# The loads of a head pair issued later, the mask adds split off, and a pair of context tiles kept in SBUF

## The chip, the cores and the metric

The kernel runs on one core of a Trainium2 chip. The time is the device time of one execution in microseconds (us); lower is better.

## What is computed

Sixteen sequences of 64 tokens with 512 features go through LayerNorm and a cross-attention over a context of the same shape (32 heads of 128), with a position bias and a mask, then a residual; then LayerNorm, a base linear map plus eight low-rank experts weighted by a router, and a residual.

```python
q = (layernorm(x) @ Wq).reshape(16, 64, 32, 128)      # k, v: ctx @ Wk, ctx @ Wv
score = einsum('bqhd,bkhd->bhqk', q, k) / sqrt(128) + position_bias
probs = softmax(where(mask, score, -inf))             # masked places are 0
x = x + einsum('bhqk,bkhd->bqhd', probs, v).reshape(16, 64, 4096) @ Wo
h = layernorm(x); w = topk weights of softmax(h @ router_W.T + router_b), by expert_map
x = x + h @ base_W.T + base_b + 2 * sum_e w_e * (h @ A_e.T) @ B_e.T
```

## The kernel before

**Arithmetic.** TensorE (PE) multiplies in a reduced format. So each fp32 operand is split into a high and a low part, and each product is three matmuls: high by high, high by low, low by high. ScalarE (ACT) makes the high parts (`wk_hi`, `co_hi`, `wo_hi`), VectorE (DVE) the low ones (`wk_lo`, `co_lo`, `wo_lo`). On top of this stands the Strassen-Winograd scheme: a block of two heads is computed as seven products, `times(n, p)` with p = 1, 2, 6, 7, 5, 3, 4, of six matmuls 128x512 each. The sums that the scheme wants of the weights are made by GpSimd (POOL) in `sums_of_b(w)` (four operations into `twk`/`twv`), those of the activations by DVE in `sums_of_a(j)` (into `sums_c`, `sums_x`).

**Stages.** Blocks n = 0 to 15 make V and are stored in HBM, blocks 16 to 31 make K likewise. From block 31 on come the Q blocks. Then sixteen rounds over pairs of heads follow (i = 0 to 15). In each, PE first does what this text calls the group of small passes: transposing the probabilities of the old pair (`turn_p`), scores of the next one (`scores`, L1544) and probabilities by V (`times_v`, L1569, output `pO`, `pT_`, `pS`). These are some 190 short matmuls with 4-byte operands. Then it does the products of Q block n = i + 33 mixed with eight output tiles `times_wo(i, t)` into `pY`, which DVE adds to the residual `y` (`add_tile`, L1101):

```python
for p in (1, 2, 6, 7): times(n, p)
times_wo(i, 0); times_wo(i, 1); times(n, 5); times_wo(i, 2); times_wo(i, 3)
times(n, 3); times_wo(i, 4); times_wo(i, 5); times(n, 4); times_wo(i, 6); times_wo(i, 7)
```

`times_wo(i, t)` with t of 2 or more waits until tile t - 2 has been added (`y_added`), because `pY` has two buffers. The engines meet only through semaphores; each engine's own order is the order in which the code is written.

**DVE in a round.** Bias and row maximum (`biased`, `largest`, `less_max`), low parts of the attention output (`oT_lo`), the row sums and scaled probabilities (`add_up`, L1131; `weights`, L1133 to L1140, whose L1135 and L1140 read two SBUF operands), the `q` combinations (L897, L903, L908), low weights (L887), and the eight `add_tile`.

**POOL in a round.** `sums_of_b(i + 22)` and then `add_mask` for the two heads of the pair after next (L581), each waiting for its bias load.

**SP in a round.** The loads, in the order `wo_raw` (after `wo_l`), `k` (after `s_full`: the scores have read the old k), eight bias pieces (each four after `s_read`), `wk_raw`, and `v` (after `o_full`: `times_v` has read the old v).

**Opening.** The eight context tiles are transposed in pairs (`turn_pair(j)`, with `rows_out(j)` on ACT making the high and low copies). The sums for index 0 (`sums_of_a(0)`) are made late, at block 5; by then the PSUM copy of tiles 0 and 4 is gone, so PE transposes them again at n = 5 (`turn(ctx[:, 0, :], ...)`, L1429), and `rows_out(0)` copies them. `ORDER` lists the first products.

**End.** Before the last pair's `times_v`, PE transposes the last weights of the FFN (`ffn_weights(6)`, L1619, `b_raw`).

## Time and profile before

| | us |
|---|---|
| median of 3 runs | 797.49 (796.79 to 798.37) |
| the profiled execution, whole | 799.1 |
| its span on the core | 797.3 |
| PE busy in the span | 781.9 (98%) |
| DVE busy | 585.0 (73%) |
| ACT busy | 335.4 (42%) |
| POOL busy | 186.6 (23%) |

The span runs from the first to the last instruction of the core; the whole execution has a little around it. Busy time counts an engine's own work, overlaps within the engine counted once. The profile of one execution gives the start and length of each instruction, and, in brackets, how long its engine had been idle and which instruction released it.

### The profile page before, as it was taken

To read this page: it belongs to the slowest core of one execution; us is meant where nothing else is said; L and a number is where in the kernel's file an instruction comes from. 1 tells how busy PE (TensorE), PEld (TensorE's weight loads), DVE (VectorE), ACT (ScalarE), POOL (GpSimd) and SP (SyncE) were. 2 spreads that over 40 slices of the span, in tenths; PEclk is the share of its full clock that TensorE was granted. 3 is DMA by queue.
4 is the path that set the end of the run, shared out by engine and by line. 5 is a ranking of instruction groups with operands and counts; after the bars stand their busy time and mean duration, and the time that the engine had idled before them with its cause. 6 is when DMAs were issued, how large, how long until landed. Compare 5 with 4: busy or idle time off the path is not lost.

```text
span 797.3 us, 16339 instructions
## 1 busy us (share of the span) xinstructions
PE 781.9 (98%) x6368; PEld 651.8 (82%) x6368; DVE 585.0 (73%) x1047; ACT 335.4 (42%) x657; POOL 186.6 (23%) x203
## 2 busy tenths in 40 slices
PE   9999999999999999989999999999999999999998
PEld 7788888888888888768888878887888788888886
DVE  6794626267677666688987888788878887869884
ACT  5563525245455555452443234423443343324420
POOL 0134041024334334242212221212221221010200
PEclk9999999999999999999999999999999999999999
DMA  6536674234544556583564355435543455344002
GB/s 224 196 121 211 214 238 145 106 142 159 186 163 159 164 165 211 168 245 107 159 186 114 103 163 179 126 105 159 170 144 114 141 160 167 93 121 101 1 3 105
DMA packets 108075, 118.35 MB, mean 148 GB/s; under 512 B 44240, under 2 KB 77008, under 8 KB 107999
## 3 DMA queue, kind: packets, MB, share of 16 engines
q1 hardware_dynamic: 107998, 117.31, 46.7%
q8 instruction: 51, 0.84, 0.4%
q14 instruction: 26, 0.20, 0.1%
HBM read 81.64 MB, written 35.65 MB: 147 GB/s over the span
## 4 chain that ended last, share of the span: by engine, by line
PE 89%; DVE 7%; DMA 2%; issue 1%; SPq 1%; ACT 0%; DVEq 0%
PE pY L1383 40%; PE pP L1383 36%; PE pY L1544 4%; PE pO L1569 2%; PE pT_ L1569 1%; DVE pr L1140 1%; DVE rs L1135 1%; DVE y L1101 1%; DVE sm L1131 1%; PE pO L1383 1%; PE pT_ L1554 1%; PE pS L1554 1%; DMA k_hbm<-stage 1%; DMA v<-v_hbm 1%; SPq L422 1%
## 5 line engine op out<-in xcount | busy, mean ns | idle before, releaser
L1383 PE MATMUL pY<-wo_hi,oT_hi 128*128 128x512 f32 x248 | 97.8, 394 | 3.6 <-DVE y L1101 2.3
L1101 DVE TENSOR_TENSOR y<-y,pY 128x512 f32<-128x512 f32 x124 | 84.7, 683 | 18.6 <-PE pY L1383 18.3
L1383 PE MATMUL pY<-wo_lo,oT_hi 128*128 128x512 f32 x248 | 96.7, 390 | 0.0
L1383 PE MATMUL pY<-wo_hi,oT_lo 128*128 128x512 f32 x248 | 96.6, 390 | 0.0
L1383 PE MATMUL pP<-xo_hi,wk_hi 128*128 128x512 f32 x210 | 83.7, 398 | 1.8 <-ACT v_s L633 0.8
L648 ACT CAST wk_hi<-twk 128x256 fp32r<-128x256 f32 x128 | 52.1, 408 | 72.6 <-PE pP L1383 61.1
L1383 PE MATMUL pP<-xo_lo,wk_hi 128*128 128x512 f32 x210 | 81.9, 390 | 0.0
L1383 PE MATMUL pP<-xo_hi,wk_lo 128*128 128x512 f32 x210 | 81.9, 390 | 0.0
L581 POOL TENSOR_TENSOR bias<-bias,madd 128x512 f32<-128x512 f32 x32 | 42.7, 1348 | 151.8 <-DMA bias<-in_fside_Bx32xSxS 151.8
L887 DVE TENSOR_TENSOR wk_lo<-twk,wk_hi 128x256 fp32r<-128x256 f32 x128 | 58.8, 464 | 23.3 <-ACT wk_hi L648 23.3
L887 DVE TENSOR_TENSOR wk_lo<-wk_raw,wk_hi 128x256 fp32r<-128x256 f32 x96 | 46.6, 486 | 21.9 <-ACT wk_hi L648 21.8
L1383 PEld LDWEIGHTS pY<-wo_hi,oT_hi 128*128 128x128 f32 x248 | 46.5, 188 | 16.4 <-DVE y L1101 5.7
L564 POOL TENSOR_TENSOR twk<-wk_raw 128x256 f32<-128x256 f32 x32 | 24.5, 764 | 129.1 <-DVE wk_lo L887 104.2
L1383 PEld LDWEIGHTS pY<-wo_lo,oT_hi 128*128 128x128 f32 x248 | 46.5, 188 | 9.8
L1383 PEld LDWEIGHTS pY<-wo_hi,oT_lo 128*128 128x128 f32 x248 | 46.6, 188 | 9.2
L575 POOL TENSOR_TENSOR twk<-wk_raw,twk 128x256 f32<-128x256 f32 x32 | 24.0, 749 | 117.7 <-DVE wk_lo L887 117.7
L1383 PEld LDWEIGHTS pP<-xo_hi,wk_hi 128*128 128x128 f32 x210 | 39.4, 188 | 12.9 <-issue 4.4
L633 ACT COPY v_s<-pP 128x512 f32<-128x512 f32 x31 | 18.2, 587 | 75.2 <-PE pP L1383 75.2
L1383 PE MATMUL pP<-co_hi,wk_hi 128*128 128x512 f32 x126 | 49.3, 391 | 0.0
L1383 PE MATMUL pP<-co_lo,wk_hi 128*128 128x512 f32 x126 | 49.0, 389 | 0.0
L1383 PE MATMUL pP<-co_hi,wk_lo 128*128 128x512 f32 x126 | 49.0, 389 | 0.0
L1383 PEld LDWEIGHTS pP<-xo_lo,wk_hi 128*128 128x128 f32 x210 | 39.4, 188 | 8.4
(277 smaller groups left out, 1916.9 us busy)
## 6 DMA issues: line engine op xcount, KB each, us to landing
v_hbm<-stage SPq DMA_DIRECT2D x64, 256.0 KB, 2.3
k_hbm<-stage SPq DMA_DIRECT2D x64, 256.0 KB, 3.5
k<-k_hbm SPq DMA_DIRECT2D x16, 1024.0 KB, 5.4
v<-v_hbm SPq DMA_DIRECT2D x16, 1024.0 KB, 7.3
wk_raw<-in_L_xattn_Wk SPq DMA_DIRECT2D x16, 512.0 KB, 4.4
wo_raw<-in_L_xattn_Wo SPq DMA_DIRECT2D x16, 512.0 KB, 3.7
bias<-in_fside_Bx32xSxS SPq DMA_DIRECT2D x128, 64.0 KB, 3.5
wk_raw<-in_L_xattn_Wq SPq DMA_DIRECT2D x16, 512.0 KB, 4.6
```

The lines of the kernel that those rows point to most:

```text
L422: sp.dma_start(bias[h % 2][64 * f:64 * f + 64, i::2, :], bias_d[f, i, h]).then_inc(ld_bias[h % 2], 16)
L564: nc.gpsimd.tensor_tensor(tw[:, 0, :, :], raw_block(w, 1, 1), raw_block(w, 0, 1), ALU.subtract).then_inc(tw_made, 1)
L575: nc.gpsimd.tensor_tensor(tw[:, 3, :, :], raw_block(w, 1, 0), tw[:, 1, :, :], ALU.subtract).then_inc(tw_made, 1)
L581: nc.gpsimd.tensor_tensor(b[:, :, :], b[:, :, :], madd[:, :, :], ALU.add).then_inc(bias_made, 1)
L633: nc.scalar.copy(v_s[:, :], x_bank(n)[:, :]).then_inc(v_made, 1)
L648: nc.scalar.copy(w_part(w, 0)[:, slot, :, :], w_source(w, slot)).then_inc(w_hi[slot], 1)
L887: nc.vector.tensor_tensor(dst, src, hi.bitcast(F32), ALU.subtract).then_inc(done, 1)
L1101: nc.vector.tensor_tensor(y[:, t, :], y[:, t, :], src[:, :], ALU.add).then_inc(y_added, 1)
L1383: mm = nc.tensor.matmul(bank_, a, b, start=first and n == 0, stop=last and n == len(terms) - 1, skip_group_check=read_between)
L1544: mm = nc.tensor.matmul(pY[s][64 * half:64 * half + 64, blk * S:(blk + 1) * S], q[:, s, b * S:(b + 1) * S], k[:, s, b * S:(b + 1) * S], st ...
L1554: mm = nc.tensor.transpose(pT_of[h % 2][:, j * P:(j + 1) * P], pr[h % 2][:, 2 * j:2 * j + 2, :].rearrange("p a k -> p (a k)"), ident[:, :])
L1569: mm = nc.tensor.matmul(pO_of[s][i][64 * d:64 * d + 64, t * S:(t + 1) * S], v[rows, t, s * DH + 64 * d:s * DH + 64 * d + 64], pT[s][rows, ...
```

## The change

The change moves work and takes a little of it away; the arithmetic is the same.

1. **Opening.** Product 5 of block 1 goes ahead of product 2 of block 2, and the DVE and ACT operations for them change places with it.
2. **Tiles 0 and 4.** Their transposed form is copied from PSUM to SBUF (`kept0`, two ACT copies) when it is first made. The second transposing (8 PE transposes), and `rows_out(0)`, go. `turn_pair(2)` waits for the copies.
3. **Before the rounds.** ACT does `copy_c12` ahead of `exp(0)`, DVE `make_c11` ahead of `weights(0)`.
4. **SP.** In a round, `wo_raw` comes first; everything else waits for `o_full`, that is for the end of the group of small passes; then `wk_raw`, the bias, `k`, `v`.
5. **POOL.** The two `add_mask` stand between the third and fourth operation of `sums_of_b`.
6. **wo.** ACT makes `wo_high(i + 1)` two steps earlier, and DVE makes `lower_wo(i + 1)` right after `add_tile(i, 1)` where it stood after `add_tile(i, 4)`.
7. **End.** `ffn_weights(6)` and its split stand behind the last pair's `times_v`.

```diff
--- before.py
+++ after.py
@@ -81,7 +81,7 @@
-ORDER = [(1, 1), (0, 2), (1, 2), (0, 4), (0, 3), (0, 7), (1, 6), (1, 7), (2, 1), (2, 2), (1, 5), (1, 3), (2, 6),
+ORDER = [(1, 1), (0, 2), (1, 2), (0, 4), (0, 3), (0, 7), (1, 6), (1, 7), (2, 1), (1, 5), (2, 2), (1, 3), (2, 6),
          (2, 7), (1, 4), (2, 5)]
 for n_ in range(3, QA + 1):
...
@@ -91,10 +91,9 @@
 DONE = {step: i + 1 for i, step in enumerate(ORDER)}
-FIRST_TURN = [0, 1, 4, 6, 10, 12, 14, 16]
-SECOND_TURN = [2, 3, 5, 7, 11, 13, 15, 17]
-AGAIN = (8, 9)
-NTURN = 18
+FIRST_TURN = [0, 1, 4, 6, 8, 10, 12, 14]
+SECOND_TURN = [2, 3, 5, 7, 9, 11, 13, 15]
+NTURN = 16
 SUM_ORDER = [1, 2, 3, 0, 4, 5, 6, 7]
@@ -200,6 +199,8 @@
         low = [at("low_c", R2, [P, DC, P]), at("low_x", R4 + 6144, [P, DC, P])]
         sums_a = [at("sums_c", R2 + 2048, [P, 4, 2, P]), at("sums_x", R4 + 8192, [P, 4, 2, P])]
+        kept0 = [at("kept0_a", R2 + 6144, [P, 2, 2, P]), at("kept0_b", R2 + 8192, [P, DC, P])]
+
         R5 = R4 + 24576
         twv = at("twv", R5, [P, 4, 2, HALF])
@@ -510,15 +511,16 @@
...
                 sp.wait_ge(wo_l, i + 1)
                 load_wo(i + 1)
+
+                sp.wait_ge(o_full, 4 * (i + 1))
+                if i + 24 < NSET:
+                    load_wk(i + 24)
                 if i + 2 < NP:
-                    sp.wait_ge(s_full, 2 * i + 4)
-                    load_k(i + 2)
                     for s in range(2):
                         sp.wait_ge(s_read, 2 * i + 3 + s)
                         load_bias(2 * i + 4 + s)
-                if i + 24 < NSET:
-                    load_wk(i + 24)
-                sp.wait_ge(o_full, 4 * (i + 1))
+                    sp.wait_ge(s_full, 2 * i + 4)
+                    load_k(i + 2)
                 load_v(i + 1)
                 if i == NP - 4:
@@ -553,7 +555,12 @@
                 b = n % NX
                 nc.gpsimd.tensor_tensor(rstd[:, b:b + 1], ve[:, b:b + 1], mhalf[:, :], ALU.pow).then_inc(rstd_made, 1)
-            def sums_of_b(w):
+            def add_mask(h):
+                pool.wait_ge(ld_bias[h % 2], 64 * (h // 2 + 1))
+                b = bias[h % 2]
+                nc.gpsimd.tensor_tensor(b[:, :, :], b[:, :, :], madd[:, :, :], ALU.add).then_inc(bias_made, 1)
+
+            def sums_of_b(w, masks=()):
                 tw = tw_of(w)
                 wait_raw(pool, w)
@@ -570,15 +577,12 @@
...
                 nc.gpsimd.tensor_tensor(tw[:, 2, :, :], raw_block(w, 0, 1), raw_block(w, 0, 0), ALU.subtract
                                         ).then_inc(tw_made, 1)
+                for h in masks:
+                    add_mask(h)
                 pool.wait_ge(w_lo[6], w)
                 pool.wait_ge(tw_made, 4 * w + 2)
                 nc.gpsimd.tensor_tensor(tw[:, 3, :, :], raw_block(w, 1, 0), tw[:, 1, :, :], ALU.subtract
                                         ).then_inc(tw_made, 1)
-
-            def add_mask(h):
-                pool.wait_ge(ld_bias[h % 2], 64 * (h // 2 + 1))
-                b = bias[h % 2]
-                nc.gpsimd.tensor_tensor(b[:, :, :], b[:, :, :], madd[:, :, :], ALU.add).then_inc(bias_made, 1)
             for n in range(QA + 1):
                 if n in (1, 5, 9):
@@ -594,11 +598,12 @@
                     rstd_of((n - 16) // 3 * 2 + 1)
             for i in range(NP):
+                heads = (2 * i + 2, 2 * i + 3) if i + 1 < NP else ()
                 if i + 22 < NSET:
-                    sums_of_b(i + 22)
-                if i + 1 < NP:
-                    add_mask(2 * i + 2)
-                    add_mask(2 * i + 3)
+                    sums_of_b(i + 22, heads)
+                else:
+                    for h in heads:
+                        add_mask(h)
             pool.wait_ge(ld_small, 48)
             for t in range(NT):
...
@@ -697,15 +702,21 @@
...
             higher(0, 2)
             piece_of_first(1, 3, pP[0], c12_made)
+
+            act.wait_ge(a21_l, 1)
+            nc.scalar.copy(kept0[0][:, :, :, :], first_turn(0)[:, :].rearrange("p (k c t) -> p k c t", k=2, c=2)
+                           ).then_inc(kept0_made, 1)
+            nc.scalar.copy(kept0[1][:, :, :], second_turn(0)[:, :].rearrange("p (c t) -> p c t", c=DC)
+                           ).then_inc(kept0_made, 1)
             piece_of_first(3, 7, pP[1], c22_made)
             first_high(2)
+            higher(0, 4)
             copy_u(1)
             rows_out(2)
             last_high(2)
-            higher(0, 4)
             copy_p1(2)
+            sums_high(2)
             copy_v(1)
-            sums_high(2)
             higher(0, 6)
             copy_c12(1)
...
@@ -736,8 +747,6 @@
...
                 if j is not None:
                     sums_high(j)
-                if n == 5:
-                    rows_out(0)
                 copy_v(n)
                 if n == 5:
...
@@ -792,8 +801,8 @@
...
             copy_v(n)
             higher(w, 4)
+            copy_c12(n)
             exp(0)
-            copy_c12(n)
             higher(w, 5)
             exp(1)
...
@@ -831,10 +840,10 @@
...
                 copy_u(n)
                 higher_of(w, 2)
+                wo_high(i + 1)
                 higher_of(w, 3)
                 copy_v(n)
                 higher_of(w, 4)
-                wo_high(i + 1)
                 copy_c12(n)
                 higher_of(w, 5)
...
@@ -854,9 +863,9 @@
...
             turned_p(h + 3)
             split_ffn(5)
-            split_ffn(6)
             o_high(h + 2)
             o_high(h + 3)
+            split_ffn(6)
             for i in range(NT + 1):
                 if i < NT:
@@ -925,7 +934,12 @@
                 low_, s, k = low[j // 4], sums_a[j // 4], SUM_ORDER.index(j)
                 one = first_turn(j)[:, :].rearrange("p (k c t) -> p k c t", k=2, c=2)
-                dve.wait_ge(low_made, k + 1)
+                if j == 0:
+                    one, low_ = kept0
+                    dve.wait_ge(kept0_made, 2)
+                else:
+
+                    dve.wait_ge(low_made, k + 1 if j < 4 else k)
                 if k >= 1:
                     dve.wait_ge(as_lo, k)
...
@@ -1029,13 +1043,13 @@
...
             lower_w(0, 2)
             make_c11(1)
-            first_low(2)
             first_t1()
             first_t4()
+            first_low(2)
             lower_w(0, 4)
             sums_of_a(2)
+            sums_low(2)
             make_c11(2)
-            sums_low(2)
             lower_w(0, 6)
             make_c22(1)
...
@@ -1180,9 +1194,9 @@
...
             add_up(0)
             lower_w(w, 6)
+            make_c11(n)
             weights(0)
             lower_w(w2, 0)
-            make_c11(n)
             add_up(1)
             lower_w(w2, 1)
...
@@ -1217,6 +1231,7 @@
...
                 weights(h + 3)
                 add_tile(i, 1)
+                lower_wo(i + 1)
                 lower_of(w, 1)
                 lower_of(w, 2)
...
@@ -1226,7 +1241,6 @@
...
                 lower_of(w, 5)
                 add_tile(i, 4)
-                lower_wo(i + 1)
                 add_tile(i, 5)
                 make_c21(n)
...
@@ -1436,8 +1450,7 @@
             def turn_pair(j):
                 if j == 2:
-                    pe.wait_ge(a6_lo, 1)
-                    pe.wait_ge(a21_l, 1)
+                    pe.wait_ge(kept0_made, 2)
                 elif j == 4:
                     pe.wait_ge(as_lo, 4)
...
@@ -1499,8 +1512,8 @@
...
             times(1, 7)
             times(2, 1)
+            times(1, 5)
             times(2, 2)
-            times(1, 5)
             times(1, 3)
             times(2, 6)
...
@@ -1514,10 +1527,6 @@
...
                 if prep_at(n) is not None:
                     turn_pair(prep_at(n))
-                if n == 5:
-                    pe.wait_ge(a6_lo, 3)
-                    turn(ctx[:, 0, :], first_turn(0))
-                    turn(ctx[:, 4, :], second_turn(0))
                 times(n, 6)
                 times(n, 7)
...
@@ -1677,9 +1686,9 @@
...
             turn_p(h + 3)
             ffn_weights(5)
-            ffn_weights(6)
             times_v(h + 2)
             times_v(h + 3)
+            ffn_weights(6)
             def turn_last(t):
                 pe.wait_ge(xn2_made, t + 1)
```

Three places show how the rows move. SP's queue in the second round, before: the loads that serve the pair after this one.

```order
L426 DMA wo_raw<-in_L_xattn_Wo 128x2x512 [waits wo_l]
L429 DMA k<-k_hbm 128x2x1024 [waits s_full]
L422 DMA bias_92<-in_fside_Bx32xSxS_0 64x4x64 [waits s_read]
L422 DMA bias_92<-in_fside_Bx32xSxS_0 64x4x64 x3
L422 DMA bias_93<-in_fside_Bx32xSxS_0 64x4x64 [waits s_read]
L422 DMA bias_93<-in_fside_Bx32xSxS_0 64x4x64 x3
L416 DMA wk_raw_99<-in_L_xattn_Wq 128x4x256 [waits tw_made,w_lo5]
L432 DMA v<-v_hbm 128x8x256 [waits o_full]
```

The same place on SP in the changed kernel.

```order
L427 DMA wo_raw<-in_L_xattn_Wo 128x2x512 [waits wo_l]
L417 DMA wk_raw_99<-in_L_xattn_Wq 128x4x256 [waits tw_made,w_lo5,o_full]
L423 DMA bias_92<-in_fside_Bx32xSxS_0 64x4x64 [waits s_read]
L423 DMA bias_92<-in_fside_Bx32xSxS_0 64x4x64 x3
L423 DMA bias_93<-in_fside_Bx32xSxS_0 64x4x64 [waits s_read]
L423 DMA bias_93<-in_fside_Bx32xSxS_0 64x4x64 x3
L430 DMA k<-k_hbm 128x2x1024 [waits s_full]
L433 DMA v<-v_hbm 128x8x256
```

`wk_raw` now goes ahead of the bias, `k` behind it, and all of them behind the wait for `o_full`.

On POOL, the sums of one weight set and the masks of one pair, before:

```order
L564 TENSOR_TENSOR twk<-wk_raw_98 128x256 [waits w_lo3,ld_wk0]
L568 TENSOR_TENSOR twk<-twk,wk_raw_98 128x256 [waits tw_made,w_lo2]
L571 TENSOR_TENSOR twk<-wk_raw_98 128x256 [waits w_lo4]
L575 TENSOR_TENSOR twk<-wk_raw_98,twk 128x256 [waits tw_made,w_lo6]
L581 TENSOR_TENSOR bias_92<-bias_92,madd 128x512 [waits ld_bias0]
L581 TENSOR_TENSOR bias_93<-bias_93,madd 128x512 [waits ld_bias1]
```

The same place on POOL in the changed kernel:

```order
L571 TENSOR_TENSOR twk<-wk_raw_98 128x256 [waits w_lo3,ld_wk0]
L575 TENSOR_TENSOR twk<-twk,wk_raw_98 128x256 [waits tw_made,w_lo2]
L578 TENSOR_TENSOR twk<-wk_raw_98 128x256 [waits w_lo4]
L561 TENSOR_TENSOR bias_92<-bias_92,madd 128x512 [waits ld_bias0]
L561 TENSOR_TENSOR bias_93<-bias_93,madd 128x512 [waits ld_bias1]
L584 TENSOR_TENSOR twk<-wk_raw_98,twk 128x256 [waits tw_made,w_lo6]
```

The fourth sum now stands behind both masks.

On DVE, the middle of a round before, from the second `add_tile` on (`y<-y,pY` is an `add_tile`, `q<-pP,v_s` is `make_c22`):

```order
L1101 TENSOR_TENSOR y<-y,pY 128x512 [waits y_full]
L887 TENSOR_TENSOR wk_lo<-wk_raw_99,wk_hi 128x256 [waits w_hi1]
L887 TENSOR_TENSOR wk_lo<-twk,wk_hi 128x256 [waits w_hi2]
L903 TENSOR_TENSOR q<-pP,v_s 128x512 [waits s_full,v_made,prod]
L887 TENSOR_TENSOR wk_lo<-twk,wk_hi 128x256 [waits w_hi3]
L1101 TENSOR_TENSOR y<-y,pY 128x512 [waits y_full]
L887 TENSOR_TENSOR wk_lo<-twk,wk_hi 128x256 [waits w_hi4]
L1101 TENSOR_TENSOR y<-y,pY 128x512 [waits y_full]
L887 TENSOR_TENSOR wk_lo<-wk_raw_99,wk_hi 128x256 [waits w_hi5]
L1101 TENSOR_TENSOR y<-y,pY 128x512 [waits y_full]
L887 TENSOR_TENSOR wo_lo_56<-wo_raw,wo_hi_55 128x1024 [waits wo_h]
```

The same place on DVE in the changed kernel:

```order
L1115 TENSOR_TENSOR y<-y,pY 128x512 [waits y_full]
L896 TENSOR_TENSOR wo_lo_56<-wo_raw,wo_hi_55 128x1024 [waits wo_h]
L896 TENSOR_TENSOR wk_lo<-wk_raw_99,wk_hi 128x256 [waits w_hi1]
L896 TENSOR_TENSOR wk_lo<-twk,wk_hi 128x256 [waits w_hi2]
L912 TENSOR_TENSOR q<-pP,v_s 128x512 [waits s_full,v_made,prod]
L896 TENSOR_TENSOR wk_lo<-twk,wk_hi 128x256 [waits w_hi3]
L1115 TENSOR_TENSOR y<-y,pY 128x512 [waits y_full]
L896 TENSOR_TENSOR wk_lo<-twk,wk_hi 128x256 [waits w_hi4]
L1115 TENSOR_TENSOR y<-y,pY 128x512 [waits y_full]
L896 TENSOR_TENSOR wk_lo<-wk_raw_99,wk_hi 128x256 [waits w_hi5]
```

`wo_lo` has moved from behind the fifth `add_tile` of the round to a place ahead of the third.

## Rows read from the trace of the kernel before

**Rows 1.** PE alone: one round, then twelve. Length, busy (count), clock, DMA share, GB/s.

```profile
402.69:428.24 25.55, 25.55 (x292) 1.00 0.50 145
376.39:690.75 314.36, 310.00 (x3482) 1.00 0.47 141
```

**Rows 2.** PE alone: 13 groups of small passes, the same columns; the sum of all.

```profile
402.69:406.73 4.04, 4.04 (x194) 1.00 0.17 23
...
663.67:668.81 5.14, 4.24 (x193) 1.00 0.36 102
...
sum 55.88, PE 53.88; mean PE 4.14
```

**Rows 3.** Timeline: PE resumes in the longest group (start, length, idle before).

```profile
668.67 0.21 PE L1569 MATMUL pS<-pT,v 64*64 64x64 f32 x1 [0.90 <-issue]
```

**Rows 4.** The page's instruction queue (packets, MB), and a stretch of all engines.

```profile
q8 instruction: 51, 0.84, 0.4%
...
665.87:665.97 0.10, 0.10 (x17) 0.10 (x16) 0.10 (x1) 0.00 (x0) 0.00 (x0) 1.00 0.70 164
```

**Rows 5.** Timeline: SP's queue in round 376.39.

```profile
378.51 0.37 SPq L429 DMA_DIRECT2D k<-k_hbm  x1
378.93 5.71 SPq L422 DMA_DIRECT2D bias<-in_fside_Bx32xSxS  x8
```

**Rows 6.** Timeline: POOL, DVE and PE in round 376.39.

```profile
385.94 2.53 POOL L581 TENSOR_TENSOR bias<-bias,madd 128x512 f32<-128x512 f32 x2 [9.84 <-DMA bias<-in_fside_Bx32xSxS]
385.97 1.27 DVE L1135 TENSOR_TENSOR rs<-rs,some 128x8 f32<-128x8 f32 x1
387.28 1.74 DVE L1140 TENSOR_TENSOR pr<-pr,rs 128x512 f32<-128x512 f32 x1
390.71 0.50 PE L1383 MATMUL pY<-wo_hi,oT_hi 128*128 128x512 f32 x1 [0.46 <-DVE y L1101]
```

**Rows 7.** Timeline: the same engines in round 402.69.

```profile
411.55 1.29 POOL L581 TENSOR_TENSOR bias<-bias,madd 128x512 f32<-128x512 f32 x1 [9.15 <-DMA bias<-in_fside_Bx32xSxS]
412.90 0.69 DVE L1140 TENSOR_TENSOR pr<-pr,rs 128x512 f32<-128x512 f32 x1
418.20 0.68 DVE L1101 TENSOR_TENSOR y<-y,pY 128x512 f32<-128x512 f32 x1
420.47 0.39 PE L1383 MATMUL pY<-wo_hi,oT_hi 128*128 128x512 f32 x1
```

**Rows 8.** Durations of wo_lo: ns min/median/max, first and last start.

```profile
L887 DVE TENSOR_TENSOR wo_lo<-wo_raw,wo_hi x16: 1219/1220/1760, 346.1 to 735.7; 128x1024 fp32r<-128x1024 f32 x16
```

**Rows 9.** Timeline of the opening.

```profile
31.73 0.47 PE L1383 MATMUL pY<-wv_hi,co_hi 128*128 128x512 f32 x1 [0.77 <-ACT v_s L633]
32.56 1.23 DVE L887 TENSOR_TENSOR co_lo<-sums_c,co_hi 128x1024 fp32r<-128x1024 f32 x1 [1.07 <-ACT co_hi L673]
32.96 0.40 PE L1383 MATMUL pY<-wv_lo,co_hi 128*128 128x512 f32 x1
33.89 0.47 PE L1383 MATMUL pP<-wv_hi,co_hi 128*128 128x512 f32 x1 [0.54 <-issue]
```

**Rows 10.** Timeline: tiles 0 and 4 transposed again, and what follows.

```profile
64.87 0.60 PE L1429 MATMUL pS<-ident,ctx 128*128 128x128 f32 x4
...
65.66 0.48 PE L1383 MATMUL pY<-wv_hi,co_hi 128*128 128x512 f32 x1
```

**Rows 11.** Timeline ahead of the rounds and in the first.

```profile
336.16 0.47 PE L1383 MATMUL pP<-xo_hi,wk_hi 128*128 128x512 f32 x1 [0.53 <-ACT stage L638]
...
341.07 0.47 PE L1383 MATMUL pP<-xo_hi,wk_hi 128*128 128x512 f32 x1 [0.48 <-DVE q L897]
...
351.22 0.29 PE L1569 MATMUL pO<-pT,v 64*64 64x64 f32 x4 [0.17 <-DMA v<-v_hbm]
...
354.88 0.50 PE L1383 MATMUL pP<-xo_hi,wk_hi 128*128 128x512 f32 x1
```

**Rows 12.** Timeline of the end.

```profile
740.00 0.47 PE L1383 MATMUL pY<-wo_hi,oT_hi 128*128 128x512 f32 x1 [1.12 <-issue]
```

More of the change, by code:

```diff
@@ L287, in xattn_ffn @@
         turned, turned_hi, turned_lo = sem("turned"), sem("turned_hi"), sem("turned_lo")
-        low_made, sum_step = sem("low_made"), sem("sum_step")
+        low_made, sum_step, kept0_made = sem("low_made"), sem("sum_step"), sem("kept0_made")
         a01_hi, a01_lo, a6_hi, a6_lo = sem("a01_hi"), sem("a01_lo"), sem("a6_hi"), sem("a6_lo")
@@ L474, in _ @@
                     for t in range(NT):
-                        sp.wait_ge(turned, 10)
+                        sp.wait_ge(turned, 8)
                         sp.dma_start(y[:, t, :], x_d[:, t, :]).then_inc(ld_x[t], 16)
@@ L656, in rows_out @@
             def rows_out(j):
-                act.wait_ge(turned, AGAIN[1] + 1 if j == 0 else SECOND_TURN[j] + 1)
+                act.wait_ge(turned, SECOND_TURN[j] + 1)
                 if j != 1:
@@ L987, in normalise @@
                     if m >= NX:
-                        dve.wait_ge(turned, 10 + m - NX + 1)
+                        dve.wait_ge(turned, 8 + m - NX + 1)
                     nc.vector.tensor_scalar(xn[:, b, :], y[:, t, :], mv[:, b, 0:1], rstd[:, b:b + 1],
```

## The prediction

> **What bounds the kernel now.** I read first the stretches of PE, since PE is the engine that is hardly ever idle. In twelve rounds, 314.36 us, it is busy for 310.00 [rows 1]. So only work taken off PE, or a wait of PE that goes, can shorten the time; DVE, ACT, POOL and the DMA queues count only where PE stands waiting for them. The granted clock is 1.00 in each of these stretches, so nothing is lost or to be won there. The round without any wait takes 25.55 [rows 1]. Twelve of those would be 306.60, so the twelve rounds hold 314.36 - 306.60 = 7.76 of waiting. Where is it?
>
> The second view is the groups of small passes. The undisturbed one issues its first part in 4.04, thirteen of them take 55.88 against 13 x 4.04 = 52.52 [rows 2]: 3.36 too much, of which 0.34 belongs to the thirteenth, after the twelve rounds. So about 3.0 of the 7.76 sits in the groups and 4.7 outside. The timeline of the rest shows the second kind in round 376.39: `wo_hi,oT_hi` at 390.71 starts after PE has been idle for 0.46, released by an addition to `y` on DVE [rows 6]. Seven of the twelve rounds have such waits.
>
> Why is `y` late? POOL adds the masks from 385.94 on for 2.53; DVE's L1135, an operation on 8 columns, starts beside it at 385.97 and takes 1.27, and L1140 takes 1.74 [rows 6]. In round 402.69 the mask comes at 411.55, after L1135, L1140 takes 0.69, and PE waits for no `y` [rows 7]. So a mask add that lies beside a DVE operation with two SBUF inputs holds it up, by up to 1.05 (1.74 - 0.69), and `add_tile(0)` and what follows are late.
>
> **Opening.** Matmuls of a product start 0.23 apart: from 31.73 to 32.96 there are five steps, the first of them 0.30 [rows 9]. A matmul shown with 0.40 thus overlaps the next by 0.17, and a wait costs its idle time, 0.17, and 0.07 for the slower first step. Two waits stand here: 0.77 for `v_s`, and one of 0.54 behind which `co_lo` (32.56 + 1.23 = 33.79) is what ends last [rows 9]. With the 0.24 each they cost 1.01 and 0.78. The new order puts product 5, whose inputs are there, into this place, and both should go: -1.8. The kept copies are two ACT operations of some 0.6 each; they fall where ACT waits for PE, before the next transposing. Were they not hidden they would cost 1.2, which is the bound. The eight transposes at n = 5 go: from 64.87 to 65.66 is 0.79 [rows 10], and with what the switch costs the next product (0.08) this is -0.9.
>
> **Before the rounds.** The waits at 336.16 (0.53, for ACT's `stage`) and 341.07 (0.48, for DVE's `q`) [rows 11] cost 0.77 and 0.72, together 1.5; ACT and DVE now do the copy and the `q` first. But `v` arrives only just ahead of 351.22, and from there to the next product at 354.88 lie 3.66 of small passes [rows 11], which a late `v` would hold in place. I take -1.3, between 0.3 (the `v` load stays where it is, only the queue behind it shortens) and 1.6.
>
> **The loads in the rounds.** `k` is issued at 378.51, inside the group (2.12 after its start), then eight bias pieces in 5.71, some 0.71 each [rows 5]. Now all of this waits for the end of `times_v`. Nobody needs `k` before the next round's scores, 25.55 after, so being late costs nothing by itself. What could it win? The 3.36 in the groups. Only every third group is long, although `k` is issued at the same place in each. In the longest, PE resumes at 668.67 after 0.90 without a releaser [rows 3], 2.7 after a short burst of the DMA engines (0.70 busy in 0.1 us) ended at 665.97. The instruction queue brings 0.84 MB in 51 packets, 16.5 KB each [rows 4]. The other long groups end 2.5 to 2.8 after such a burst as well, at whatever other traffic. I read this as PE's own code arriving late, on a rhythm set by the number of instructions, and take 0 from the loads. The bounds are -3.4, if the loads were what delays the code, and +1, if 16 fewer PE instructions move the rhythm into a worse place.
>
> The Trainium skill, "Runtime: NRT & Kernel Launch", section "Instruction fetch mechanics", says that code comes in 16 KiB blocks of 256 instructions, that PE holds 128 KiB, and that crossing a block is mostly hidden. The packet size here agrees with the block; by "mostly hidden" the gaps would need another cause, the loads would be the first suspect, and the sum would be lower by the 3.4 of the row; by the rows I leave it out.
>
> **The masks.** With the bias starting 2.5 after the group's start, the masks came 9.5 (385.94 - 376.39) and 8.9 (411.55 - 402.69) after it [rows 6, 7]. Now the group must end (4.04 at least, [rows 2]) and `wk_raw` goes first (about 0.5), so the bias starts some 2.0 later and the first mask lands 10.9 to 11.6 after the start, the second 1.5 later. `weights(h + 2)` on DVE ends at 412.90 + 0.69, which is 10.9 after the start: the first pair of DVE operations is free, and the second (`weights(h + 3)`) can still be met. That would clear most of the 4.7. But there is a new load on DVE ahead of the third addition: `wo_lo`, 1.22 [rows 8]. In the clean round that addition ends at 418.20 + 0.68 = 418.88, and PE wants it at 420.47 [rows 7]: a margin of 1.59, of which 0.37 is left. One contention of 1.05 against 0.37 makes 0.68 of waiting, and I expect it in something under half of the rounds: 0.3 a round, 3.6 in twelve. Against 4.7 that is -1.1. The lower bound is no waits at all, -4.7; the upper is in the rivals. The fourth POOL sum, now behind the masks, feeds weights that DVE takes later in the round, past the tile additions. ACT's earlier `wo_high` is work that ACT, 42% busy, has room for; that `wo_raw` is free earlier only lets its load go earlier.
>
> **End.** `ffn_weights(6)` before `times_v` is four transposes, about 0.45; behind them PE waits 1.12 at 740.00 anyway [rows 12]. Moved into that wait they are free: -0.45.
>
> **The sum.** -1.8 - 0.9 - 1.3 + 0 - 1.1 - 0.45 = -5.55. The profiled execution took 799.1 (span 797.3), so it would take 793.5; it lies 1.6 above the median of the runs, and the same edits on the median of 797.49 give **791.9**.
>
> **The rivals.**
>
> *A, the loads do delay the code.* For it: the longest group has the DMA engines busy for 0.36 of its time, the short ones 0.17 [rows 2]. Against it: in a longer window more of `k` is bound to show, and two of three groups pass with the same issues. It takes a further 3.4: 788.5; with clean additions too, 784.9.
>
> *B, the masks meet DVE, and `wo_lo` has eaten the margin.* Ends on the other side. If the bias lands sooner than I think, so that the first mask begins before 9.8 after the group's start, where `weights(h + 2)` has its turn, both L1135 and L1140 are held (1.1 and 1.05, [rows 6]). Before, this cost up to 26.3 - 25.55 = 0.75 a round; now a further 1.22 stands in front of the third addition. I price it at 1.2 a round, between 0.75 and 0.75 + 1.22. Twelve rounds give 14.4 for 4.7, +9.7 in place of -1.1: 797.49 - 4.45 + 9.7 = 802.7. It decides the sign from 4.7 + 4.45 = 9.15 in twelve rounds, 0.76 a round. Against it: the 2.0 by which the chain of issues moves is sure, except in the last rounds, which have no `wk_raw` ahead.
>
> *C, the gains of opening and setup are given back.* Another input, DVE's low weights or `v`, ends the same waits a little later: half of 1.8 and 1.0 of the 1.3 go, and masks still cost what they did (1.1): 791.9 + 3.0 = 794.9; with the kept copies in the way (1.2), 796.1.
>
> **How the numbers follow.** Forecast 0.50, with a range of its own of 790 to 793.9; A 0.17; C 0.18, of which a third ends within 0.2% of before; B 0.15, of which a fifth ends within 0.2%. A measurement of this kernel can tell 0.2%, 1.6 us, from no change. Faster than 795.9: 0.50 + 0.17 + 0.12 = 0.79, less 0.03 for terms that miss together: 0.76. Within: 0.06 + 0.03 + 0.03 = 0.12. Slower than 799.1: 0.12. The range takes in most of A (down to 786.5) and C and its neighbours (up to 798); B above it and the far end of A are left out.
>
> **What would show it.** Opening: no PE wait longer than 0.2 between the products of blocks 1 and 2, and the start of the K blocks earlier by 2.7. The transposes at n = 5 missing. Rounds: first mask 10.9 to 11.6 after the group's start, L1140's successor near 0.69 for the first head, PE's waits for `y` adding up to 3 to 4 in twelve rounds, most of them ahead of the fifth tile. Groups: every third still long by 0.4 to 1.1, 2.5 to 2.8 after a 16.5 KB burst; if they are all 4.04 long, A holds and my reading of the code fetch is wrong. End: the wait at 740.00 shorter by the four transposes. The prediction fails high if `wo_lo` proves to be waited for in every round, and low if the groups go clean.

## The result, and the profile after

The changed kernel is slower: 805.13 us median (804.93 to 807.83, 4 runs) against 797.22 of the kernel before beside it, a ratio of 1.0105, 95% interval 1.0081 to 1.0129. Forecast was 791.9, with a range up to 798.0. The profiled execution has a span of 803.4.

The page: busy time of the engines, and the first matmuls of the output tiles (the last column is PE's idle time ahead of them and what ended it).

```profile
PE 782.9 (97%) x6360; PEld 649.8 (81%) x6360; DVE 586.2 (73%) x1047; ACT 334.9 (42%) x658; POOL 198.7 (25%) x203
...
L1397 PE MATMUL pY<-wo_hi,oT_hi 128*128 128x512 f32 x248 | 99.2, 400 | 7.4 <-DVE y L1115 6.6
```

The engines do the same work, but PE now waits 7.4 ahead of its output tiles, 6.6 of it for `y`. The stretches of PE (start and end, length, busy (count), clock, DMA share, GB/s): the twelve rounds, and of thirteen groups of small passes some, with their sum.

```profile
374.01:694.80 320.79, 312.58 (x3481) 1.00 0.45 138
...
374.01:378.05 4.04, 4.04 (x193) 1.00 0.02 4
...
507.73:512.75 5.02, 4.36 (x194) 1.00 0.02 5
...
694.80:699.43 4.63, 4.30 (x194) 1.00 0.01 4
sum 55.69, PE 53.71; mean PE 4.13
```

Against [rows 1] the twelve rounds take 320.79 - 314.36 = 6.43 more. Against [rows 2] the groups take 55.69 for 55.88: nothing changed there, although the DMA engines now stand nearly still in them (4 to 8 GB/s where there were 18 to 102). So the loss is between the groups. The span reads as follows, against the kernel before: up to the first scores 327.69 for 330.60, -2.91; from there to the first of the twelve rounds 46.32 for 45.79, +0.53; twelve rounds +6.43; round 14 26.17 for 25.88, +0.29; from 720.97 to the end 82.43 for 80.67, +1.76. The sum is 6.1, the difference of the spans.

One of the rounds, that of 481.17, by timeline (POOL, DVE, then PE):

```profile
490.50 1.30 POOL L561 TENSOR_TENSOR bias<-bias,madd 128x512 f32<-128x512 f32 x1 [15.20 <-DMA bias<-in_fside_Bx32xSxS]
490.75 1.07 DVE L1149 TENSOR_TENSOR rs<-rs,some 128x8 f32<-128x8 f32 x1
494.21 1.73 POOL L561 TENSOR_TENSOR bias<-bias,madd 128x512 f32<-128x512 f32 x1 [2.41 <-DMA bias<-in_fside_Bx32xSxS]
495.30 1.72 DVE L896 TENSOR_TENSOR wo_lo<-wo_raw,wo_hi 128x1024 fp32r<-128x1024 f32 x1
495.90 1.72 POOL L584 TENSOR_TENSOR twk<-wk_raw,twk 128x256 f32<-128x256 f32 x1
496.95 0.95 DVE L896 TENSOR_TENSOR wk_lo<-wk_raw,wk_hi 128x256 fp32r<-128x256 f32 x1
499.09 0.68 DVE L1115 TENSOR_TENSOR y<-y,pY 128x512 f32<-128x512 f32 x1
499.82 0.50 PE L1397 MATMUL pY<-wo_hi,oT_hi 128*128 128x512 f32 x1 [0.71 <-DVE y L1115]
```

The reader is to see three meetings. The first mask meets L1149 (the former L1135), 9.3 after the group's start, where I had forecast 10.9 to 11.6. The second mask meets `wo_lo`, and so does the fourth POOL sum behind it: `wo_lo` takes 1.72 where 1.22 is its length alone [rows 8]. The same sum then meets `wk_lo`, which takes 0.95 for 0.42. Behind all this stands the third addition (499.09), and PE waits for it ahead of the fifth output tile. In the kernel before, seven of the twelve rounds have a wait for `y`, all ahead of the third or fourth tile and none ahead of the fifth. Now 13 rounds (the first to the thirteenth) wait ahead of the fifth, with PE idle for 0.14 to 0.94, and three of them also ahead of the third or fourth, for 0.31 to 0.56.

The other rounds look alike, with one difference: where the second mask comes early enough to meet the second head's L1149 or L1154 (the former L1140), `wo_lo` has its 1.22, and where it comes later, `wo_lo` is held (1.62 to 1.81, in eight of the thirteen rounds from the second on). L1154 of the first head is held in none of them: it takes 0.69 in each.

### The profile page after: what moved, and what is told of

Read it like the earlier page. It is cut to its first block, busy times and chain, and to the rows that moved or that the text cites. A ratio compares the mean times of both kernels' runs of the same rounds, so it can differ in the third digit from the quotient of the medians.

```text
span 803.4 us, 16325 instructions
## 1 busy us (share of the span) xinstructions
PE 782.9 (97%) x6360; PEld 649.8 (81%) x6360; DVE 586.2 (73%) x1047; ACT 334.9 (42%) x658; POOL 198.7 (25%) x203
## 4 chain that ended last, share of the span: by engine, by line
PE 86%; DVE 10%; issue 2%; DMA 1%; ACT 1%; SPq 0%; DVEq 0%
PE pY L1397 37%; PE pP L1397 37%; PE pY L1553 4%; DVE wk_lo L896 2%; DVE wo_lo L896 2%; DVE y L1115 2%; PE pO L1578 2%; PE pT_ L1578 1%; DVE q L912 1%; DMA wv_raw<-in_L_xattn_Wv 1%; PE pO L1397 1%; PE pT_ L1563 1%; PE pS L1563 1%; PE pS L1578 1%; DVE st L966 1%
## 5 line engine op out<-in xcount | busy, mean ns | idle before, releaser
L561 POOL TENSOR_TENSOR bias<-bias,madd 128x512 f32<-128x512 f32 x32 | 44.5, 1392 | 247.8 <-DMA bias<-in_fside_Bx32xSxS 247.8
L896 DVE TENSOR_TENSOR wk_lo<-wk_raw,wk_hi 128x256 fp32r<-128x256 f32 x96 | 48.3, 504 | 9.3 <-ACT wk_hi L653 9.1
L1397 PEld LDWEIGHTS pP<-xo_hi,wk_lo 128*128 128x128 f32 x210 | 39.4, 188 | 8.1 <-issue 0.4
```

The costliest lines, as they stand in the source:

```text
L561: nc.gpsimd.tensor_tensor(b[:, :, :], b[:, :, :], madd[:, :, :], ALU.add).then_inc(bias_made, 1)
L896: nc.vector.tensor_tensor(dst, src, hi.bitcast(F32), ALU.subtract).then_inc(done, 1)
L1397: mm = nc.tensor.matmul(bank_, a, b, start=first and n == 0, stop=last and n == len(terms) - 1, skip_group_check=read_between)
```

## The experiments

Each stands beside runs of the kernel before on the same chip. "Outside" means the changes in the opening, ahead of the rounds and at the end; the times are medians.

**e1, the changes outside the rounds alone.** Of the diff: `ORDER`, `kept0`, the order ahead of the rounds, `ffn_weights(6)`; SP, POOL and wo as before.

> The kernel before with the changes outside the rounds alone (opening, kept tiles, the order ahead of the rounds, the end); SP, POOL and wo as before. In the trace of the changed kernel the first group of scores started 2.9 us earlier. Theory (the loss is made inside the rounds, by POOL's mask adds and wo_lo on DVE): 794 to 796, and rounds with 4 to 5 us of waits for y in twelve, none ahead of the fifth output tile. Rival (the shift of everything, or the shifted rhythm of PE's code, makes the loss): 800 or more.

796.67, ratio 1.0002 (0.9984 to 1.0020), between the theory and its rival. As forecast there are no waits ahead of the fifth tile, and the first scores start at 327.93. But little of that reaches the end. Of ten runs nine lie between 794.2 and 799.9 (the tenth took 1110; without it the median is 795.93). Something takes most of the gain back; see e8.

**e2, the changes inside the rounds alone.**

> The kernel before with the three changes inside the rounds alone (order on SP, place of the masks on POOL, place of wo). Theory: the twelve rounds lose 6.4 us as in the changed kernel, and the opening gives nothing back: 803.5 to 807. Rival (shift): near 797.

805.25, ratio 1.0108 (1.0092 to 1.0124), as forecast. The loss is made in the rounds; the shift falls.

**e3, wo back.**

```diff
@@ ACT, the round
-                wo_high(i + 1)
                 higher_of(w, 3)
...
                 higher_of(w, 4)
+                wo_high(i + 1)
@@ DVE, the round
                 add_tile(i, 1)
-                lower_wo(i + 1)
...
                 add_tile(i, 4)
+                lower_wo(i + 1)
```

> The changed kernel with wo_high and lower_wo at their old places; loads and masks stay moved. Theory: the waits ahead of the fifth output tile (7.6 us and some 1.4 for restarts in 13 rounds) go nearly all, the ones ahead of the third stay (about 2.5): 796 to 798.5. Rival (the later loads or the masks alone cost it, wo_lo has no part): 803 to 805.

795.61, ratio 0.9987 (0.9962 to 1.0011). This one edit takes back all of the loss. I had also expected the waits ahead of the third tile to stay; no wait for `y` is left at all, although the first mask still meets L1149 in nine of the twelve rounds (which then takes 0.92 to 1.28). Twelve rounds of PE, by stretches:

```profile
373.29:683.37 310.08, 308.21 (x3482) 1.00 0.47 143
```

**e4, wo alone moved (with the changes outside).**

> The changed kernel with SP's order and POOL's masks as before; only wo moved (and the changes outside the rounds). Theory: masks meet DVE as in the kernel before, and behind them wo_lo makes the third addition late, in the rounds where the masks meet DVE about 0.5 more each: 798 to 801. Rival (wo_lo harmless without the late loads): 794 to 796, the same as e1.

799.04, ratio 1.0027 (1.0001 to 1.0053), inside the forecast and 2.4 above e1. So an early `wo_lo` costs in company of the old masks too, but about a third of what it costs with the moved ones (7.5, below).

**e5, thin masks.** The kernel leaves out the mask in 448 of the 512 columns of each bias block.

```diff
-                nc.gpsimd.tensor_tensor(b[:, :, :], b[:, :, :], madd[:, :, :], ALU.add).then_inc(bias_made, 1)
+                nc.gpsimd.tensor_tensor(b[:, 0:1, :], b[:, 0:1, :], madd[:, 0:1, :], ALU.add).then_inc(bias_made, 1)
```

> The changed kernel, with each mask add done on 64 of the 512 columns (the other columns keep the bias without the mask): POOL meets DVE for some 0.2 us where it met it for 1.3. Theory (late additions need both, the contention and wo_lo ahead of the third): waits for y nearly gone, the twelve rounds 313 at most, 796 to 799. Rival (wo_lo alone makes the third addition late): the waits ahead of the fifth output tile stay at 0.3 to 1.0 a round, over 802.

790.55, ratio 0.9921 (0.9907 to 0.9935), below the 796 to 799 of the theory. Everything else is the changed kernel, `wo_lo` in front included, and no round waits for `y`:

```profile
373.78:682.58 308.80, 307.37 (x3481) 1.00 0.46 144
```

Twelve times 25.55 are 306.60; the 2.2 left are the long groups. It shows that an early `wo_lo` (and ACT's early `wo_high`) without the full masks is harmless: its 1.22 fits into the margin of 1.59, as I had worked out. In the twelve rounds the mask adds cost the changed kernel 320.79 - 308.80 = 11.99. The medians, each less its kernel before, lie 14.5 apart; a part of the rest has another source: the changed kernel's stop of PE in round 15 (see e8) is missing from this execution, though it too is 16 PE instructions short.

```profile
708.57:714.44 5.87, 5.87 (x201) 1.00 1.02 209
```

**e6 and e7, SP's order back; POOL's order back.**

> The changed kernel with SP's old order in the rounds (k and bias inside the group, wk behind). Theory: the masks come 8.6 to 9.9 after the group's start as in the kernel before, meet weights of the first head, and wo_lo is still ahead of the third addition: like e4, 798 to 802, between e4 and the changed kernel because the fourth POOL sum still stands behind the masks. Rival (the later loads are what costs): 794 to 797.

> The changed kernel with POOL's masks back behind the fourth sum. Theory (POOL's fourth sum, pushed behind the masks, meets wo_lo and the low weights and adds to the delay): 802 to 804, rounds 6, 7, 9 and 12 lose less. Rival (place on POOL means nothing): 804.5 to 806.

Both lie inside their forecasts. e6: 799.85, ratio 1.0033 (1.0018 to 1.0049), like e4. e7: 802.25, 1.0053 (1.0029 to 1.0077), spread from 797.8 to 805.2. Taken with the changed kernel, the later loads make most of the difference once wo is early, the fourth POOL sum behind the masks some of it. e7's spread allows no finer statement.

**e8, e3 and 16 more PE instructions.** A count of 16 is what the changed kernel lost with the transposes of tiles 0 and 4 (eight matmuls and their eight weight loads).

```diff
-            warm_up(8)
+            warm_up(16)
```

> e3 (wo at its old place) with 8 more warm-up transposes at the very start, where PE waits for the first context tile: 16 more PE instructions, as many as the changed kernel lost. Theory (PE's long groups follow the count of its instructions): groups are long in the rounds in which they were in the kernel before (4, 7, 10, 13, 14), the group of round 15 takes 5.9 and not 8.1, and the median falls by 2 to 792 to 794. Rival (the stall in round 15 comes from the loads): the same groups as e3, 795 to 797.

794.84 (793.37 to 796.60, 11 runs), ratio 0.9972 (0.9961 to 0.9983). Against the kernel before it is 2.3 lower where e3 was 1.4 lower. The fall of 0.9 is less than the 2 of the forecast; but e3's runs reach from 792.1 to 802.0. The long groups went back to where they were in the kernel before, rounds 4, 7, 10 and 13, and the group of round 15 is short again. Round 15's group, first in the changed kernel, then in e8:

```profile
720.97:729.08 8.11, 6.13 (x201) 1.00 0.80 172
```

```profile
712.05:717.92 5.87, 5.87 (x202) 1.00 0.98 203
```

**e9, e1 and the same 16.**

> e1 (the changes outside the rounds alone) with 8 more warm-up transposes at the start, so that PE's instruction count before the rounds is that of the kernel before. Theory: round 15's group takes 5.9 and not 8.4, the spread of the times narrows as in e8, and the gain outside the rounds shows: 793.5 to 795, 3 below before (2.7 of opening, the end 0.5, little ahead of the rounds). Rival (the opening's gain is lost elsewhere): 796 to 797.5.

794.61 (793.32 to 795.66, 12 runs), ratio 0.9973 (0.9962 to 0.9984). What the changes outside the rounds are worth is 2.2; in e1 most of it was hidden.

**e10, the kernel before with 16 PE instructions fewer** (`warm_up(14)` made `warm_up(6)`).

> The kernel before with 8 warm-up transposes fewer (6 where there were 14), nothing else. Theory (the count of PE instructions sets which groups are long, and round 15 gets a long one at full DMA load): groups long in rounds 4, 7, 10, 11, 14, 15, the times spread over 5 us or more, the median 1 to 3 above before (798 to 800). Rival (warm-ups mean nothing): 796.5 to 797.5, round 15's group 5.9.

799.08 (795.30 to 806.26, 12 runs), ratio 1.0032 (1.0009 to 1.0055): 8 transposes less work, and slower. That is inside the forecast, and the groups of rounds 11 and 15 became long, as forecast. In round 15 PE stops, and then its clock falls (stretches of PE; in each the number behind the count is the granted clock):

```profile
714.40:724.28 9.88, 7.65 (x202) 0.79 0.83 203
...
720.00:722.00 2.00, 2.00 (x38) 0.54 0.78 235
...
724.00:726.00 2.00, 2.00 (x6) 0.50 0.63 220
...
728.00:730.00 2.00, 2.00 (x11) 1.00 0.00 0
```

PE had been idle for 2.23, ending at 719.21:

```profile
719.21 0.27 PE L1569 MATMUL pS<-pT,v 64*64 64x64 f32 x1 [2.23 <-issue]
```

The clock of the next stretches is 0.54 and 0.50, that is the level of 1.2 GHz and not 2.4; six matmul starts in 2 us where eleven are usual. Such executions are the upper end of the spread: the profiled one took 802.1.

**e11, the changed kernel and the same 16.**

> The changed kernel with 8 more warm-up transposes at the start. Theory: only the last round's stall goes: 802 to 803.5, the waits for y as in the changed kernel. Rival (the shift has a part in the waits for y): below 800.

801.93 (801.10 to 802.79, 4 runs), ratio 1.0066 (1.0046 to 1.0086). It is 5.2 above the kernel before (796.77 on this chip) where the changed kernel is 7.9 above: 2.7 of the loss go with the lost 16 instructions. Not all of that is shown to be round 15: in the profiled executions its group takes 5.86 for 8.11, but the twelve rounds, too, take 2.25 less than the changed kernel's 320.79:

```profile
374.83:693.37 318.54, 312.95 (x3482) 1.00 0.45 139
```

**e12, k ahead of the bias.**

```diff
                 if i + 2 < NP:
+                    sp.wait_ge(s_full, 2 * i + 4)
+                    load_k(i + 2)
                     for s in range(2):
                         sp.wait_ge(s_read, 2 * i + 3 + s)
                         load_bias(2 * i + 4 + s)
-                    sp.wait_ge(s_full, 2 * i + 4)
-                    load_k(i + 2)
```

> The changed kernel with k issued ahead of the bias (behind wk), so that k's megabyte stands ahead of the bias on the queues as in the kernel before. Theory (the masks came earlier than forecast because k no longer delayed the bias): first mask 10.9 to 12 after the group's start instead of 9.3 to 9.9, weights of the first head are met no more; the waits ahead of the third output tile go, those ahead of the fifth stay in the rounds where a mask meets wo_lo or the second head's weights: 799 to 803. Rival (what the masks meet does not matter, the order of loads does not move them): 804.5 to 806.

806.01, ratio 1.0121 (1.0093 to 1.0148): no faster than the changed kernel (1.0081 to 1.0129), against the forecast of 799 to 803. The masks did come later, 11.9 to 14.9 after the group's start in rounds 2 to 12. Round 373.96:

```profile
386.61 1.29 POOL L561 TENSOR_TENSOR bias<-bias,madd 128x512 f32<-128x512 f32 x1 [18.56 <-DMA bias<-in_fside_Bx32xSxS]
387.18 1.79 DVE L896 TENSOR_TENSOR wo_lo<-wo_raw,wo_hi 128x1024 fp32r<-128x1024 f32 x1
388.90 1.51 DVE L896 TENSOR_TENSOR wk_lo<-wk_raw,wk_hi 128x256 fp32r<-128x256 f32 x1
392.87 0.50 PE L1397 MATMUL pY<-wo_hi,oT_hi 128*128 128x512 f32 x1 [0.98 <-DVE y L1115]
```

The first head's weights are met no more and no wait stands ahead of the third tile. But `wo_lo` and the low weights behind it are now held by both masks (0.57 and 1.09 more), and PE waits ahead of the fifth tile in ten of twelve rounds, in nine of them idle for 0.90 to 1.48. The two without a wait are those in which the first mask came only when `wo_lo` was done (14.7 after the start, `wo_lo` from 13.2 to 14.5). So where the mask falls is not what matters most; that `wo_lo` is there to be met is.

**e13, late masks and wo at its old place** (e12's order on SP, e3's edit, e8's 16).

> wo at its old place, k ahead of the bias, 8 more warm-up transposes, the rest as changed. Theory (late masks harm only through wo_lo): masks 12 to 15 after the group's start, there beside low weights that have a margin; waits for y in twelve rounds under 0.5, 792.5 to 794.5, at or below e8 and e9. Rival (late masks also hold the low weights, and through them the third addition): 795 to 799.

792.25 (791.55 to 792.79, 5 runs), ratio 0.9940 (0.9928 to 0.9952): faster than both kernels, with a narrow spread, and just below the forecast. Its twelve rounds by stretches:

```profile
375.17:684.43 309.26, 307.84 (x3481) 1.00 0.50 143
```

And the masks of the round of 375.17 in the timeline, with what lies beside them on DVE:

```profile
387.24 3.24 POOL L561 TENSOR_TENSOR bias<-bias,madd 128x512 f32<-128x512 f32 x2 [17.95 <-DMA bias<-in_fside_Bx32xSxS]
...
388.40 0.92 DVE L896 TENSOR_TENSOR wk_lo<-wk_raw,wk_hi 128x256 fp32r<-128x256 f32 x1
389.24 1.52 DVE L896 TENSOR_TENSOR wk_lo<-twk,wk_hi 128x256 fp32r<-128x256 f32 x1
```

The masks still hold DVE, by 0.5 and 1.1, but without `wo_lo` the margin takes it: PE is idle for no `y` in the twelve rounds. So the aim of the change, masks that come later, was worth having with `wo` left where it was: each against its kernel before, e13 is 2.2 better than e8.

**e14 and e15, b_raw loaded later.** The four loads of `b_raw`, whose small packets fill the DMA engines in round 15, issued behind the last pair's v.

> e10 with the loads of b_raw (four with many small packets) issued behind the last pair's v, after round 15's group. Theory (in round 15 the code waits behind b_raw's packets on full DMA engines, and PE's clock falls after the gap): round 15's group 5.9 to 6.6, clock 1.00, times within 3 us, 796 to 797.5. Rival (the stall needs only the count of instructions, whatever the traffic): group 8 to 10 and a median near 799.

> As e13 without the extra warm-ups, but with b_raw loaded behind the last pair's v. Theory: the stall in round 15 goes the other way, 792 to 794.5, narrow spread. Rival (a late b_raw is waited for by its transposes, or the stall stays): 795 to 798.

e14: 800.58 (796.25 to 803.69), ratio 1.0040 (1.0019 to 1.0061). e15: 795.76 (794.07 to 797.75), ratio 0.9987 (0.9976 to 0.9997). The stop stayed in both, so my theory of `b_raw`'s packets fell. In e14 PE resumes here in the timeline:

```profile
718.60 0.27 PE L1570 MATMUL pS<-pT,v 64*64 64x64 f32 x1 [2.44 <-issue]
```

And three stretches of PE, up to it, in it and around its end:

```profile
714.00:716.00 2.00, 2.00 (x113) 1.00 1.02 394
716.00:718.00 2.00, 0.15 (x11) 1.00 0.07 23
718.00:720.00 2.00, 1.40 (x61) 1.00 0.04 8
```

PE stands for 2.44 while the DMA engines are busy for 0.07 of the time. But up to the stop they are full with other loads (1.02), so e14 takes `b_raw` out of the question and not all traffic. What the profiled executions do show is this. With the old count of instructions (the kernel before, e2, e8, e9, e11, e13) none of six stops in round 15; with 16 fewer, nine of eleven do, for 1.93 to 2.44, and e4 and e5 do not. So the count is needed for the stop and is not enough for it. e14's own edit also costs something: behind the group, PE waits 1.39 for `b_raw` (at 729.29).

## Why the prediction was wrong, step by step

**Opening: right.** -2.7 was forecast, the first scores start 2.91 earlier, and both waits of [rows 9] are gone. That is not one lucky pair of traces: in the four profiled executions with the old opening the first scores start at 330.01 to 331.11, in the nine with the new one and no added warm-up at 327.52 to 328.01.

**Before the rounds: mis-sized.** -1.3 was forecast; the stretch up to round 1 is 17.69 for 18.05, -0.36, and from the first scores to round 2 nothing of it is left. Three waits of the changed kernel:

```profile
334.71 0.47 PE L1397 MATMUL pP<-xo_hi,wk_hi 128*128 128x512 f32 x1 [0.63 <-DVE stage L917]
...
341.17 0.47 PE L1397 MATMUL pP<-xo_hi,wk_hi 128*128 128x512 f32 x1 [0.77 <-ACT v_s L638]
...
346.57 0.28 PE L1553 MATMUL pY<-k,q 128*64 128x64 f32 x2 [0.51 <-DVE q L917]
```

And one of the kernel before:

```profile
344.83 0.47 PE L1383 MATMUL pP<-xo_hi,wk_hi 128*128 128x512 f32 x1 [0.77 <-ACT v_s L633]
```

At both places of [rows 11] PE no longer waits. But one product behind the first, PE now waits 0.63 for another operation of DVE (`stage`), the scores of round 1 wait 0.51 for DVE's `q`, and the 0.77 for `v_s`, which I had not looked at, stands in both kernels. I asked what ended the two waits, and not what would stop PE next. The first part alone is near the bottom of my bounds (0.3). From the first scores to round 2 it is 46.32 for 45.79 in the changed kernel, where round 1 already pays for the moved `wo_lo`, and 45.62 in e9, where the rounds are the old ones: -0.17. This is the part of rival C that concerns the setup.

**The loads and the groups: right for the twelve rounds, and the bound was too narrow.** The groups did not change, with the DMA engines busy for 0.01 to 0.04 of the time where it was 0.13 to 0.37, and rival A is refuted by it. But I had bounded the effect of 16 fewer PE instructions by +1, from the 0.4 to 1.1 of the long groups in [rows 2]. It came to +2.7 (the changed kernel against e11, each less its kernel before), and a part of it is that the shifted rhythm makes the group of round 15 long too, by 2.2 in the profiles at full clock, while in some executions the clock falls behind it. Here the Trainium skill, "Runtime: NRT & Kernel Launch", section "Instruction fetch mechanics", with its blocks of 256 instructions, fits what e8 to e11 show, that a small shift of the count moves the long groups. If the gaps are such crossings, its "mostly hidden" does not hold in these dense groups: 0.3 to 1.1 each, and about 2 in round 15. That the missing thing is code is still inferred, since no row names the releaser.

**The masks: the step that failed.** I forecast -1.1 in the rounds, from "10.9 to 11.6 after the start" and from "one contention of 1.05 against 0.37 makes 0.68 of waiting, and I expect it in something under half of the rounds". Both were wrong. The first mask came at 9.3 to 9.9 in nine of thirteen rounds, because I carried over the delay from issue to mask (6.3 to 7.0), and in that delay k's megabyte had stood ahead of the bias; with k behind, it was 4.6 to 5.0 in eleven of the thirteen, and with k ahead again (e12) 6.1 to 9.3. The bias itself was issued when I had said, 4.6 after the group's start in round 481.17:

```profile
485.78 5.21 SPq L423 DMA_DIRECT2D bias<-in_fside_Bx32xSxS  x8
```

The second error weighs more. That early masks alone are harmless is seen in e3, that late ones do not help while `wo_lo` is there in e12. I counted DVE's own chain as one contention against the margin of 0.37, in under half of the rounds. But `wo_lo` is itself an operation with two SBUF inputs, and so are the low weights behind it. By moving it ahead of the third addition, the change put 1.22 of work there and also two or three more things for POOL to hold. Of the fourth POOL sum I had asked only who needs its result, and not what it holds while it runs: it lies beside `wo_lo` and `wk_lo`. In each of the thirteen rounds at least two of DVE's operations ahead of the third addition were held. The term was to cost 3.6 in twelve rounds; the parts between the groups took 291.27 for 284.36 in thirteen. Thirteen clean ones would be 279.63, so that the 4.7 of waiting of before became 11.6.

**Rival B came nearest, and its number is in part luck.** It gave 802.7; e11, which is the changed kernel with the rhythm restored, is 801.93. It had the sign, the early mask and the eaten margin right. But of its two held operations L1154 of the first head was free in every round, since the second mask now came 2.5 to 4.1 behind the first; the time was lost on the second head, `wo_lo` and `wk_lo` instead. And e12 has no early mask and is no faster. Its sum also takes 4.45 for the changes outside the rounds, where e9 shows 2.2, and 14.4 of waiting in twelve rounds where 11.6 were measured in thirteen: two errors of opposite sign. I gave it 0.15 because I trusted the forecast of the masks' time.

**End: right.** -0.45 was forecast; from the last pair's transposes to its first output product it is 4.62 for 5.06, -0.44.

By medians, each less its kernel before: changes outside the rounds -2.2 (e9), moved loads and masks without wo -0.2 (e8 less e9: -2.3 and -2.2), wo on top of them +7.5 (e11 less e8: 5.2 and -2.3), 16 fewer instructions +2.7. The sum is the +7.9 of the result, but the parts depend on the order in which they are taken: the 16 instructions are worth 0.9 between e3 and e8, 1.8 between e1 and e9, 2.3 in e10 and 2.7 in e11, and `wo` without them 9.3 (the changed kernel against e3).

## What to carry to other kernels

When an operation is moved up on an engine ahead of one that is waited for, its price is its length only if nothing can hold it; here an operation with two SBUF inputs beside one POOL operation of 1.3 us took up to 1.15 us longer, whatever its own length (0.17 became 1.32, 0.42 became 1.51, 0.69 became 1.74), and the test is to thin out the POOL work (e5) before sizing the move. A delay from issue to arrival belongs to the queue that stood there and is read anew when the order changes. Where a kernel loses or wins a handful of PE instructions, compare it also with the count restored: a change of 16 was worth 0.9 to 2.7 us here and had hidden most of a gain of 2.2.

## What the runs showed of the hardware that was not expected

Taking out eight transposes of the warm-up, with nothing else changed, made the kernel 2.3 us slower (e10), and the profiled execution had a stop of PE of 2.2 us in one group 700 us later. After such a stop the granted clock was down to 0.50 for some microseconds in five of the nine profiled executions that have one (e10, after 2.23 idle; e6, e7, e12, e15) and 1.00 in the other four (e14, after 2.44 idle). The length of the stop does not decide: 1.93 was enough in e12, 2.27 was not in e1. What decides was not found, nor why the stop in round 15 is twice as long as in other rounds; the DMA engines are full ahead of each of these stops (busy for 0.98 or more), which was not varied.
